# GpSimd scales the attention outputs in VectorE's place, and queries and keys are projected 256 columns at a time

## The reference

```python
q = (norm(x) @ Wq + bq)          # 256 x 128 for a sequence, layer 1 rotates q and k by position
k = (context @ Wk + bk)          # 512 x 128
v = (context @ Wv + bv)
p = softmax(q k^T / sqrt(8))     # for each head, 256 x 512
x = x + (p v) @ Wo + bo
```

## Time and profile before

| | |
|---|---|
| runs | 703.84, 708.71, 710.87 us; median 708.71 |
| span of the profiled execution | 702.5 us; a time of its own is not given beside it |
| TensorE, VectorE, ScalarE, GpSimd busy | 93%, 74%, 57%, 59% |
| attention of layer 0, of layer 1 | about 40 to 231 us, 406 to 603 us |
| granted TensorE clock, mean | 0.993 of full |

### The profile page before, as it was taken

One profiled execution on the slowest core, in us unless ns is written; L12 is line 12 of the kernel. 1 busy time (PEld: TensorE's weight loads), 2 busy tenths in 40 slices (PEclk: granted clock), 3 DMA queues, 4 the chain that ended last, 5 costly groups with the idle time before them and its releaser, 6 DMA issues.

```text
span 702.5 us, 14212 instructions
## 1 busy us (share of the span) xinstructions
PE 655.6 (93%) x5301; PEld 347.0 (49%) x5301; DVE 520.6 (74%) x933; ACT 400.3 (57%) x568; POOL 412.5 (59%) x613
## 2 busy tenths in 40 slices
PE   5989999999989999999999998999999999798897
PEld 3333433443333667666656533434434343465886
DVE  4798999999898784734645578989999898374444
ACT  2067777777778525323232277777777778354342
POOL 4445657766422356879845585687787543456254
PEclk9999999999999999999999999999999999799999
DMA  6735644643400676685943125655563723114311
GB/s 183 204 107 151 155 137 101 177 133 97 108 3 2 149 175 143 159 161 183 205 103 89 48 77 125 178 159 134 152 179 112 184 84 101 32 35 128 110 36 38
DMA packets 66601, 84.97 MB, mean 121 GB/s; under 512 B 7776, under 2 KB 48624, under 8 KB 65024
## 3 DMA queue, kind: packets, MB, share of 16 engines
q1 hardware_dynamic: 63856, 79.44, 43.9%
q0 software_dynamic: 1760, 3.62, 1.6%
q10 hardware_dynamic: 916, 1.00, 0.6%
HBM read 57.57 MB, written 25.80 MB: 119 GB/s over the span
## 4 chain that ended last, share of the span: by engine, by line
PE 75%; ACT 13%; DVE 4%; issue 2%; POOL 2%; DMA 1%; another core or an unknown queue 1%; SPq 0%; ACTq 0%; DVEq 0%; POOLq 0%
PE pair L502 12%; ACT prob L935 11%; PE misc L515 8%; PE outs L629 8%; PE outs L515 7%; PE pair L363 6%; PE pair L463 6%; PE pair L365 6%; PE pair L364 6%; PE misc L416 3%; PE outs L401 2%; DVE negmax L1222 2%; PE outs L727 2%; PE misc L526 1%; PE outs L447 1%
## 5 line engine op out<-in xcount | busy, mean ns | idle before, releaser
L1222 DVE TENSOR_REDUCE negmax<-pair 128x2 f32<-128x1024 f32 x256 | 306.5, 1212 | 37.3 <-PE pair L463 32.6
L935 ACT ACTIVATE prob<-pair 128x1024 f32<-128x1024 f32 x256 | 260.3, 1025 | 92.2 <-PE pair L502 86.1
L502 PE MATMUL pair<-qstack,kstack 54*128 54x256 bf16 x1024 | 100.4, 274 | 20.8 <-ACT prob L935 19.2
L463 PE MATMUL pair<-kstack,qstack 51*128 51x512 bf16 (+1 forms) x512 | 98.1, 379 | 1.7 <-issue 0.9
L1456 DVE TENSOR_TENSOR hid<-pair,silu 128x512 f32<-128x512 f32 x68 | 46.7, 688 | 69.5 <-PE pair L365 50.7
L502 PEld LDWEIGHTS pair<-qstack,kstack 54*128 54x128 bf16 x1024 | 30.0, 94 | 125.9 <-ACT prob L935 100.6
L1082 ACT ACTIVATE silu<-pair 128x512 f32<-128x512 f32 x68 | 40.6, 599 | 87.8 <-PE pair L365 84.0
L515 PE MATMUL misc<-prob,vaug 128*32 128x256 f32 x1024 | 81.9, 395 | 3.0 <-ACT prob L935 2.8
L515 PE MATMUL outs<-prob,vaug 128*32 128x256 f32 x1024 | 83.4, 390 | 0.0
L629 PE MATMUL outs<-hid,down 128*128 128x512 f32 x136 | 70.0, 596 | 0.7 <-POOL hid L1888 0.5
L363 PE MATMUL pair<-xT,eh 128*128 128x512 f32 x136 | 70.3, 517 | 0.0
(11 more groups left out here) (290 smaller groups left out, 1093.3 us busy)
## 6 DMA issues: line engine op xcount, KB each, us to landing
kstack<-k_terms SPq DMA_DIRECT2D x30, 384.0 KB
w_here<-w_rows SPq DMA_DIRECT2D x32, 256.0 KB, 4.9
w_there<-w_rows SPq DMA_DIRECT2D x32, 256.0 KB, 5.3
k_terms<-kparts SPq DMA_DIRECT2D x16, 384.0 KB, 2.6
qstack<-q_terms SPq DMA_DIRECT2D x30, 192.0 KB, 3.6
ctx_nat<-in_ctxT SPq DMA_DIRECT2D x16, 256.0 KB, 3.3
k_terms<-kparts SPq DMA_DIRECT2D x16, 256.0 KB, 2.9
w_nat<-in_L_gu SPq DMA_DIRECT2D x9, 352.0 KB, 4.0
```

The lines of the kernel that those rows point to most:

```text
L463: return nc.tensor.matmul(to, qstack[n % 3][rows, g, qt * P:(qt + 1) * P], kstack[n % 3][rows, g, :], start=True, stop=True)
L502: e = nc.tensor.matmul(bank[m + r][:, k * SQ:(k + 1) * SQ], kstack[n % 3][rows, g, (c + k) * P:(c + k + 1) * P], qstack[n % 3][rows, g, :] ...
L935: nc.scalar.activation(prob[:, quad % 2, 2 * g:2 * g + 2, c:c + 2, :].rearrange("p j c q -> p j (c q)"), pair[t_pair(n, step)][:, :, :], A ...
L1222: nc.vector.tensor_reduce(negmax[:, n % 2, 2 * g:2 * g + 2, qt], pair[score_pair(n, step)][:, :, :], AX.X, ALU.max, negate=True).then_inc( ...
```

## The change

`q_project` becomes one product of 256 columns, all in step 0. `k_project` takes 256 columns in step 12 and 256 in step 14, and none in steps 11 and 13. `normalise_output` is parted in periods: VectorE keeps the reciprocal (step 4), GpSimd multiplies, in layer 0 behind the queries' parts, in layer 1 between the keys' parts and the queries' rotation, after waiting for the reciprocal. VectorE's `turn_normalised`, which waits for the multiply, goes from step 5 to step 7. The last output of each layer is still scaled by VectorE. Exponentials, scores and values are as they were.

```diff
--- before.py
+++ after.py
@@ -437,17 +437,13 @@
                 e.then_inc(x_turned, 1)
                 left[m] = xq_copied, n + 1
 
-            def q_project(n, m=M, parts=(0, 1)):
+            def q_project(n, m=M):
 
                 pe.wait_ge(w_scaled, n // B + 1)
                 pe.wait_ge(xq_copied, n + 1)
                 bank_free(m)
-                for i in parts:
-                    tok = slice(i * P, (i + 1) * P)
-                    e = nc.tensor.matmul(bank[m][:, tok], wnat[:, 0, :], xqT[:, tok], start=True, stop=True)
-                if i == 1:
-                    e.then_inc(q_projected, 1)
-                    left[m] = q_copied, n + 1
+                nc.tensor.matmul(bank[m][:, 0:SQ], wnat[:, 0, :], xqT[:, :], start=True, stop=True).then_inc(q_projected, 1)
+                left[m] = q_copied, n + 1
 
             def stacks_in(n, g):
                 if n == 0 and g < PAIRS // 2:
@@ -557,8 +553,8 @@
 
                     m = rest(step)
                     if 0 <= b < B - 2:
-                        if step in (0, 1):
-                            q_project(n + 2, M if n == B else m, (step,))
+                        if step == 0:
+                            q_project(n + 2, M if n == B else m)
                         if step in (5, 6, 7, 8):
                             v_project(n + 2, m, step - 5, step - 4)
                     if b >= 0 and step == 4:
@@ -567,8 +563,8 @@
                         o_project(n - 1, m)
                     if b + 1 < B and step == 10:
                         max_turn(n + 1, 0, m)
-                    if 0 <= b < B - 3 and step in (12, 13, 14):
-                        k_project(n + 3, m, step - 11, step - 10)
+                    if 0 <= b < B - 3 and step in (12, 14):
+                        k_project(n + 3, m, step - 12, step - 10)
                     if 0 <= b < B - 3 and step == 15:
                         x_turn(n + 3, m)
                     if b >= 1 and step == 14 and not early(n - 1):
@@ -595,8 +591,6 @@
 
                     if b >= 2 and step == 3 and early(n - 2):
                         y_turn(n - 2, m)
-                    if 0 <= b < B - 3 and step == 11:
-                        k_project(n + 3, m, 0, 1)
 
             def logits(blk, m, tiles=range(BT)):
                 pe.wait_ge(rt_lo, 1)
@@ -876,6 +870,11 @@
             for c in range(1, KC):
                 values(LAYERS * B - 1, 3, c)
             ffn_1()
+
+        def scale_output(engine):
+
+            engine.tensor_tensor(o_norm[:, :, :, :].rearrange("p b k v -> p k b v"), o_found[:, :, :, 0:HD],
+                                 rsum[:, :, :].unsqueeze(3).to_broadcast([P, QUADS, BLOCKS, HD]), ALU.mult).then_inc(o_normed, 1)
 
         def exchange_k(engine, waiting, n):
 
@@ -1228,14 +1227,15 @@
                 ve.wait_ge(o_normed, n)
                 nc.vector.transpose(o_found[:, 2 * half:2 * half + 2, :, :].rearrange("p k b v -> p (k b v)"), bank[outputs(half)]).then_inc(o_turned, 1)
 
+            def invert_sums(n):
+                ve.wait_ge(o_turned, 2 * n + 2)
+                nc.vector.reciprocal(rsum[:, :, :], o_found[:, :, :, HD]).then_inc(rsum_set, 1)
+
             def normalise_output(n):
-                found = o_found[:, :, :, :]
-                ve.wait_ge(o_turned, 2 * n + 2)
-                nc.vector.reciprocal(rsum[:, :, :], found[:, :, :, HD]).then_inc(rsum_set, 1)
+                invert_sums(n)
                 ve.wait_ge(rsum_set, n + 1)
                 ve.wait_ge(o_norm_turned, n)
-                nc.vector.tensor_tensor(o_norm[:, :, :, :].rearrange("p b k v -> p k b v"), found[:, :, :, 0:HD],
-                                        rsum[:, :, :].unsqueeze(3).to_broadcast([P, QUADS, BLOCKS, HD]), ALU.mult).then_inc(o_normed, 1)
+                scale_output(nc.vector)
 
             def turn_normalised(n):
 
@@ -1277,8 +1277,8 @@
                     if b >= 1 and step == 3:
                         turn_output(n - 1, 1)
                     if b >= 1 and step == 4:
-                        normalise_output(n - 1)
-                    if b >= 1 and step == 5:
+                        invert_sums(n - 1)
+                    if b >= 1 and step == 7:
                         turn_normalised(n - 1)
                     if b >= 1 and step == 10:
                         add_output(n - 1, rest(9))
@@ -1827,6 +1827,11 @@
                 pool.wait_ge(y_turned, n)
                 normalise(n, 2, y_normed)
 
+            def normalise_output(n):
+                pool.wait_ge(rsum_set, n + 1)
+                pool.wait_ge(o_norm_turned, n)
+                scale_output(nc.gpsimd)
+
             def split_y(n):
 
                 cols = slice((n % B) * SQ, (n % B + 1) * SQ)
@@ -1849,6 +1854,9 @@
                                     rope_k(n + 2, i)
                             for i in range(4):
                                 parts_of_k(n + 2, i)
+                    if b >= 1 and step == (1 if layer else 3):
+                        normalise_output(n - 1)
+                    if 0 <= b < B - 2:
                         if step == 2:
                             if layer:
                                 for i in range(3):
```

## The result

The changed kernel takes 713.76 us (median of 6 runs, 709.54 to 715.63) against 707.54 of the kernel before (6 runs, 702.87 to 710.87): ratio 1.0101, 95% interval 1.0069 to 1.0133. It is about 7 us slower, between 4.9 and 9.4; 5.5 us and a time of 714.2 were predicted. Its profiled execution took 711.73 us.

The account below looks back on a forecast made before the run. The alternation of exponential and transposed scores on one pair of banks was taken to bound the kernel. Wide projections +5.1 us and the last period +0.4 made +5.5, giving 714.2 us on the median of 708.71; range 706 to 720.

Parts of the forecast that it names:

- What counts is how much projection stands in one step, not in the period: All steps: one narrow projection just fills the 1.51 us alternation of exponential and transposed scores; two overfill it.
- the ring of 1.51 us: Exponential and transposed scores alternate on one pair of banks, so a step without projection still takes 1.51 us.
- Part 1: Wide query and key projections in both layers: 3.04 us in layer 0 and 2.02 in layer 1, +5.1 us.
- One of its signs: Wide projections on TensorE: the 256-column instructions would start 0.21 us apart.
- moving a product between them changes nothing: Layer 1, b = 0, steps 0 and 1: already past the ring with down products, so the queries add 0.
- +0.19 was counted: Queries' wide product in steps 0 and 1: +0.21 − 0.02 us a period, layer 0's b = 0 included.
- The absorption at the heads: Layer 1, heads of b = 1 and 2: TensorE's idle takes up 0.38 and 0.45 us of the longer periods before.
- Part 2: Multiply moved from VectorE to GpSimd in 14 periods: costed at zero but for +0.4 us in layer 1's last period.
- the last period's 0.4: Layer 1's last period: three token gathers now stand before VectorE's transpose, making TensorE's output projection late, +0.4 us.
- the slack of the split: Layer 1, b = 3: GpSimd's split of the maxima ends 0.8 us later, still 0.5 us ahead of TensorE's turn.
- TensorE's turn: Layer 1, b = 3: TensorE turns the split maxima at 497.92, and 0.2 us later once step 0 is longer.

Follow-up runs that it names:

- e1: Kernel before with only the wide projections, the multiply left on VectorE in step 4 and the transpose in step 5: 711.00 us, ratio 1.0099.
- e3: Kernel before with all 512 columns of the keys projected in step 12, none in 11, 13 and 14: 712.33 us, ratio 1.0087.
- e11: Kernel before with scores and transposed scores taking three pairs of banks in rotation, run beside e12 on one chip: 698.02 us, ratio 0.9897.
- e12: Changed kernel with three pairs of banks in rotation and the last period's transpose in step 5: 701.12 us, ratio 0.9894 to the kernel before.
- e9: Changed kernel with VectorE's transpose in step 5, ahead of the gathers, in layer 1's last period: 698.47 us, ratio 1.0104 to the kernel before.
- e2: Kernel before with only the multiply moved to GpSimd and the transpose to step 7, projections still 128 columns: 707.79 us, ratio 1.0039.
- e8: e2 with the multiply done three times over on GpSimd: 694.27 us, ratio 1.0035.
- e10: e12 with GpSimd's multiply behind the queries' parts in layer 1, instead of ahead of their rotation: 698.00 us, ratio 1.0103 to the kernel before.
- e4: Kernel before with the multiply done twice on VectorE, same values written again: 708.44 us, ratio 1.0053.
- e6: Kernel before with three pairs of banks in rotation and the multiply on GpSimd, projections of 128 columns: 684.39 us, ratio 0.9873.
- e7: Changed kernel with three pairs of banks in rotation: 681.19 us, ratio 0.9889 to the kernel before.
- e5: Kernel before with scores and transposed scores taking three pairs of banks in rotation, nothing else changed: 682.31 us, ratio 0.9862.

## Why the prediction was right

**What bounds the kernel.** "What counts is how much projection stands in one step, not in the period": shown by e1 and e3, which moved columns without adding any, and in reverse by e11 and e12, where the ring of 1.51 us is gone and the same move gives time.

**Part 1.** Step 12 at 1.74 us and the relieved steps at 1.51 came as worked out. One of its signs failed: the two instructions of a wide product start 0.32 us apart, not 0.21. The step came out even so, since the two narrow ones start 0.21 apart in the same place, not 0.11: half of the 0.20 fixed lies between the two instructions and half behind them. Two errors of size lie in the periods b = 0 and cancel. In layer 1 "moving a product between them changes nothing" failed: step 0 went from 1.85 to 2.06 us, while step 1 stayed at 2.06, so the product could be added but not taken away. In layer 0, step 0 of b = 0 stayed at 1.51, where +0.19 was counted. The absorption at the heads held in this pair of profiles: the earlier trace rows had 0.84 and 0.54 us of idle, and b = 1 and 2 grew by 0.02 together, with their heads, where 0.31 was predicted. It is not a fixed amount: in e9, where this code is the same, the heads of b = 2 and 3 take 2.30 and 2.59 us for the 1.83 and 1.75 here. Without the stretch at the low clock, part 1 is 2.90 us in layer 0 and 1.81 in layer 1: 4.7 for the predicted 5.1.

The Trainium skill (Perfetto Trace Analysis, Matmuls) says that larger matmuls are more efficient than smaller ones when possible. The runs show both sides: with one pair of banks for the transposed scores the larger ones cost 1% (e1), with three pairs in rotation they save 0.35 us a period of layer 0.

**Part 2.** Costed at nothing but the last period's 0.4; that term measured 0.36 and e9 took it away. The other steps of e2 are those of the kernel before, as said there. The multiply took 0.63 us on GpSimd, not the 0.73 taken, and the slack of the split was 0.98 us, not 0.5. TensorE's turn came 0.19 later behind the head of b = 3, as the prediction had it; the split ended 0.30 later, not 0.8, since the multiply holds GpSimd for 0.59 us until its next start and GpSimd reached it 0.31 us earlier behind the head. With the multiply alone (e2) the slack is 0.55. e8 found where the slack ends, e10 the other slack, that of the transpose.

The Trainium skill (GPSIMD Engine Reference, Engine selection) advises VectorE for elementwise work. The trace agrees with that against VectorE undisturbed, 0.63 against 0.42 us or 1.5 times, and hardly against VectorE's median here, 0.66; in this place neither engine's time was on the path.

**What the sum left out.** The intervals of the runs are wider than the terms. A straight line through the runs of the changed kernel, of e1 to e4 and of the kernel before beside these, time against the mean granted clock with an own level for each kernel, gives 5 us for 0.01 of clock, and these differences to the kernel before: the change +6.6 (± 1.6), wide alone +5.4 (± 1.5), the multiply alone +1.2 (± 1.2). The predicted +5.5, +5.1 and +0.4 lie inside each. What this takes off e2 and the change rests on the clock being the cause, which no run tested. The point forecast hit the median more closely than it deserved. It stood on a median of 708.71 for the kernel before, which is 707.54 with three more runs, and the difference of the medians is 6.2 us for the predicted 5.5. Of the 7.9 us in the profiled account 1 us is the clock in b = 0, and 1.9 us lie behind the last exponential, where neither part has a term; e1, with the same projections, has that stretch 1.7 us shorter than the kernel before, so it is scatter between executions.

## What to carry to other kernels

Where two engines alternate on one buffer, every step has a floor, and work is free up to it: spread side work so that each step just fills, and don't gather it in fewer, larger pieces. If you want to gather it, give the ring another buffer first. When a step moves to another engine, ask what queues behind its consumer: here 0.63 us of GpSimd cost nothing in one place and 3.5 to 5.4 us a period a few instructions later, with the stretch at the low clock that the wait brought.

## What the runs showed of the hardware

**The granted clock falls for a few microseconds, and the scatter of the runs goes with it.** TensorE in the stretches about the last exponential, kernel before, then near 45 us, kernel after (stretch, its length, busy time and count of PE, PEld, DVE, ACT and POOL, clock, DMA share, GB/s):

```profile
598.30:601.30 3.00, 0.80 (x16) 0.23 (x8) 0.42 (x1) 1.34 (x3) 2.30 (x3) 1.00 0.15 45
601.30:611.60 10.30, 8.90 (x33) 5.76 (x34) 3.97 (x11) 3.27 (x5) 3.09 (x5) 0.50 0.06 19
```

```profile
40.00:45.40 5.40, 3.46 (x34) 1.21 (x30) 5.29 (x10) 3.98 (x5) 3.66 (x8) 1.00 0.49 157
45.40:48.80 3.40, 3.18 (x26) 0.92 (x22) 2.39 (x3) 1.84 (x4) 2.73 (x5) 0.50 0.00 0
```

0.50 is 1.2 GHz, the lower of the two levels. In both TensorE was busy for 0.27 and 0.64 of the stretch ahead of it, against 0.93 in the whole. In the second, steps 3 to 5 take 5.50 us instead of 4.56. Another fall, at 549.7 us in e6, lasted 10.2 us and followed a stretch in which TensorE was busy for 7.92 of 9.7 us. e10 gives the clearest case: the same fall in five periods of five, each behind a stretch of some 4 us in which TensorE was busy for 1.2 to 2.2. The profile of the kernel before has none near 45 us, nor have those of e4 to e7, e10 and e11; e1, e2, e3, e8, e9 and e12 do. What decides between them wasn't tried.

**Chips differ in one place.** In each profile of the two chips with the kernel before at 706 us, steps 13 and 14 of the last period take 1.80 to 1.88 and 2.90 to 3.65 us; on the other two chips 0.90 and 1.20 to 1.21. What follows the last exponential takes 98.7 to 102.5 us in the profiles of the first two chips and 89.2 to 90.0 on the others, where the code is the same. 3 and 10 us make nearly the whole difference of some 14. Windows that begin 40.6 us behind the last exponential, before and e5:

```profile
642.50:662.50 20.00, 16.76 (x119) 15.52 (x120) 8.46 (x21) 7.28 (x17) 7.88 (x9) 1.00 0.35 102
```

```profile
631.90:651.90 20.00, 20.00 (x150) 19.26 (x149) 10.33 (x26) 8.64 (x21) 8.10 (x9) 1.00 0.37 107
```

Both are at full clock; TensorE is idle for 3 us of these 20 on the one chip and not on the other. In the kernel before about 5 us of the 10, an estimate, are the 10.3 us at half the clock above. Besides, there are waits whose releaser is given as "remote", which means that the profile has no instruction for the signal that ended them. The longest one of the kernel before:

```profile
DVE x L1476 <- remote: 5.5, 1, 5.5
```

Each profile of the two chips at 706 us has 3 to 7 such waits, 8 to 22 us in all, every one from step 14 of layer 1's last period on; the six profiles of the other two have none. What stands behind them no run here tells. The record doesn't name the chip of the changed kernel's profile and of the first one of the kernel before; both show the slower picture and are counted with it.
